# A transformer layer with routed experts: the loads of the first two tile pairs moved ahead of a block boundary

## The chip, the cores and the metric

The kernel runs on one core of one Trainium2 chip. The metric is the device time of one execution in microseconds (us), as the median of several runs.

## What is computed

One layer over 8 batches of 512 rows of 256 numbers: attention with 16 heads, then a feed-forward part with 16 experts, of which each row takes two, and a shared gated network. Cut to what matters here:

```python
x = x + layernorm(attention(layernorm(x)))
n = layernorm(x)
shared = (silu(n @ sfc1.T) * (n @ sfc2.T)) @ sfc3.T
top_w, top_idx = top_k(n @ gate_w.T, 2)          # per row
top_w = softmax(top_w)
dispatch[t, top_idx[t]] += top_w[t]
h = silu(einsum('td,ehd->teh', n, w1))           # 16 experts, 128 hidden
moe = einsum('teh,te,edh->td', h, dispatch, w2)
x = x + layernorm(moe + shared)
```

## The kernel before, in words

The program is three blocks, one after the other. In each, the five engines run their own lists of instructions and meet only by semaphores. Between two blocks stands a barrier (line 715): each engine drains, reports, and goes on when all five have reported.

1. The attention block.
2. The merged stage (lines 1032 to 1418). It projects the attention's result, normalises, computes the gate and the ranks of the rows, and does the first five batches of the shared network. Each row is written twice, once per chosen expert, into `records` in HBM (`rows_in` in the code), sorted by expert: a record is 256 numbers, the row's weight and its destination. GpSimd writes them with indirect scatters (`scatter`, lines 1095 to 1110), 64 in all, and waits for them at line 1123. When the counts are known, SP pads the end of each expert's region with one tile of empty records: 16 DMAs out of `pad` at line 1084, at addresses read from `counts_i`. Its last wait (line 1086, `zeroed`) is for their landing. VectorE makes the tables with the expert and the first record of every tile (`tables_i`, line 1285); from then on they are in SBUF. The stage ends with the last pieces of the shared network on TensorE and ScalarE's copy of two banks into `O` (`keep`, line 1145).
3. The expert stage (lines 1420 to 1792). 80 tiles of 128 records are taken in 40 pairs, both tiles of a pair side by side. For pair s SP loads the two tiles from `records` into `rows[s % 9]` (line 1483), at addresses from `tables_i`, which it reads 16 at a time (line 1478). TensorE transposes pair s + 1 (line 1750), ScalarE rounds it (line 1569), VectorE takes the rest (line 1669), and TensorE multiplies with the first expert weights (line 1768). TensorE reads its own table of experts, 16 at a time, at line 1743, in the step after the first transposes. Silu, another transpose and the second product (line 1780) follow, ScalarE scales the result (line 1583), and GpSimd scatters it to `rows_out` (line 1518). The last three batches of the shared network and the closing normalisation come behind it. SP waits at line 1487 until all scatters have landed before it reads them back.

The order of the work around the change is that of SP's list: 16 paddings, the wait for them, the barrier, a load of 16 registers, then the row loads of pairs 0 to 8 with no wait, and from pair 9 on each pair behind the scatter of the pair nine before it (`sent`). The tiles `rows[0]` to `rows[4]` lie in the memory of `projected`, `rows[5]` to `rows[8]` in memory of their own (`m_rows`). The first 2048 columns of `projected`'s memory hold the output projection, the gate's weights and the bias during the merged stage, and the constants of the ranks stand behind them.

```python
            sp.wait_ge(weights_in, 16 * B)
            sp.wait_ge(zeroed, 16 * E)
```

Of the kernel before, what the change touches and what calls it, by code (L numbers as in the profile page):

```python
# [5 lines left out]
B, N, D, H, HD = 8, 512, 256, 16, 16  # L6
P = 128
# [3 lines left out]
ROW = D + 2  # L11
# [7 lines left out]
RECORDS = E * REGION + E * P  # L19
# [9 lines left out]
F32 = mybir.dt.float32  # L29
# [707 lines left out]
def tiles(T, b):  # L737
    return T[:, b * QT:(b + 1) * QT, :]
# [7 lines left out]
def feed_forward(nc, ctx, iota_in, upper_in, split, rows_in, rows_out, out, X, O_rows, ident, pad, before):  # L746
# [3 lines left out]
    def sb(name, shape, dt=F32):  # L750
        return ctx.enter_context(nc.sbuf_tensor(name, shape, dt))

    def sem(name):
        return ctx.enter_context(nc.semaphore(name))
# [20 lines left out]
    pairs = projected[:, :, :, :].rearrange("p k c n -> p (k c n)")  # L775
# [7 lines left out]
    def part(T, c0, n):  # L783
# [16 lines left out]
    gate_s, lt_s, lg_s, gap_s, ratio_s, taken_s, route_s, both_s, wts_s, rank_s, slot_s = (  # L800
        asem(x) for x in "gate lt lg gap ratio taken route both wts rank slot".split())
    first_rows, copied, scattered = ([asem(f"{x}{i}") for i in range(2)] for x in ("first_rows", "copied", "scattered"))
    total_s, summed_s, table_s, end_s, inverse_s, counts_s, turned_s, zeroed, weights_in = (
        asem(x) for x in "total summed table end inverse counts turned zeroed weights_in".split())
# [223 lines left out]

    experts = sb("experts", [P, S1 // P, 2, P], F32R)
    tables_i = sb("tables_i", [2, TILES], I32)  # L1030

    with ExitStack() as sub:

# [27 lines left out]
        def sync(sp):  # L1061
            sp.dma_start(upper, upper_in).then_inc(consts_in, 16)
            sp.dma_start(iota[:, :], iota_in).then_inc(consts_in, 16)
            whole = whole_of(experts)
            for b in range(B):
                if b == B - 1:
                    sp.wait_ge(gate_s, B - 2)
                sp.dma_start(whole[:, 2 * b:2 * b + 2], split_v[:, 2 * b:2 * b + 2]).then_inc(weights_in, 16)
                sp.wait_ge(x2_s, (b + 1) * QT)
                sp.wait_ge(wts_s, b + 1)  # L1070
                if b == 0:
                    sp.wait_ge(consts, 3)
                for i in range(2):
                    t = b * QT + 2 * i
                    if b > 0:
                        sp.wait_ge(scattered[i], 32 * b)
                    sp.dma_start(second_rows[i][:, :, 0:D], O[:, t:t + 2, :]).then_inc(copied[i], 16)
                    sp.dma_start(second_rows[i][:, :, D:ROW], extra[:, t:t + 2, :]).then_inc(copied[i], 16)
            sp.wait_ge(counts_s, 1)
            at_r = [sp.alloc_register(name=f"count_at{e}") for e in range(E)]  # L1080
            sp.load(at_r, counts_i[0:1, :])
            for e in range(E):
                at = sp.snap(at_r[e], min_val=e * REGION, max_val=(e + 1) * REGION - P)
                sp.dma_start(rows_in[bass.ds(at, P), :], pad[:, :]).then_inc(zeroed, 16)
            sp.wait_ge(weights_in, 16 * B)
            sp.wait_ge(zeroed, 16 * E)

        def gpsimd(pool):
            nc.gpsimd.iota(O_rows[:, :, D + 1:ROW].bitcast(U32), pattern=[[P, NT], [0, 1]], base=0, channel_multiplier=1).then_inc(consts, 1)
# [240 lines left out]
        def tensor(pe):  # L1330
# [83 lines left out]
            for m in range(2 * LAST, EARLY * SC):  # L1414
                first(m)
                second(m - 1)
            second(EARLY * SC - 1)
        run_block(nc, sync=sync, gpsimd=gpsimd, scalar=scalar, vector=vector, tensor=tensor)

    with ExitStack() as sub:  # L1420
# [5 lines left out]
        msem = lambda name: sub.enter_context(nc.semaphore("m_" + name))  # L1426
        PAIRS = TILES // 2
        LOADS, HELD = 9, 4
        loaded, sent = ([msem(f"{x}{i}") for i in range(LOADS)] for x in ("loaded", "sent"))
        xt_s, xhi_s, xlo_s, mh_s, pre_s, msilu_s, gt_s, ghi_s, glo_s, my_s, scaled_s = (  # L1430
            msem(x) for x in "xt xhi xlo h pre silu gt ghi glo y scaled".split())
        x_out, added, pair_s, whole_s, res_s, last_out, shifted = (msem(x) for x in "x_out added pair whole res last_out shifted".split())
# [36 lines left out]
        def all_sent(engine):  # L1469
            for i in range(LOADS):  # L1470
                engine.wait_ge(sent[i], sends(i))

        def sync(sp):
            AT = 16
            at_r = [sp.alloc_register(name=f"row_at{j}") for j in range(AT)]
            for s in range(PAIRS):
                if 2 * s % AT == 0:
                    sp.load(at_r, tables_i[1:2, 2 * s:2 * s + AT])
                if s >= LOADS:
                    sp.wait_ge(sent[s % LOADS], 32 * (s // LOADS))  # L1480
                for f in range(2):
                    at = sp.snap(at_r[(2 * s + f) % AT], min_val=0, max_val=RECORDS - P)
                    sp.dma_start(rows[s % LOADS][:, f, :], rows_in[bass.ds(at, P), :]).then_inc(loaded[s % LOADS], 16)
            for b in ROWS[:ADDED]:
                sp.dma_start(out_v[b], tiles(X, b)).then_inc(x_out, 16)
            sp.wait_ge(my_s, PAIRS)
            all_sent(sp)
            for j, b in enumerate(ROWS):
                sp.dma_start(picked[:, j, :, :], moe_v[0, b]).then_inc(loaded[j], 16)
                if j < PLAIN:  # L1490
                    sp.dma_start(second[:, j, :, :], moe_v[1, b]).then_inc(loaded[j], 16)  # L1491
            for j in range(ADDED, B):
                for h in range(2):
                    at = ROWS[j] * QT + 2 * h
                    sp.wait_ge(res_s, 2 * (j - ADDED) + h + 1)
                    sp.dma_start(out_v[ROWS[j]][:, 2 * h:2 * h + 2, :], X[:, at:at + 2, :]).then_inc(last_out, 16)
            sp.wait_ge(last_out, 16 * 2 * (B - ADDED))
# [202 lines left out]
        def tensor(pe):  # L1700
# [82 lines left out]
            for i in range(EARLY, B):  # L1783
                pe.wait_ge(lo_s, (i - EARLY + 1) * DC)
                first(i * SC)
                for n in range(1, SC):
# [3 lines left out]
                    second(i * SC + n - 1)  # L1790
                second(i * SC + SC - 1)
        run_block(nc, sync=sync, gpsimd=gpsimd, scalar=scalar, vector=vector, tensor=tensor)


def transformer_layer(nc, x, w_qkv, w_out, b_out, gate_t, experts_t, cos, sin, ident_in, iota,
                      upper, steps, rows128, rows_in, rows_out, out):
    with ExitStack() as ctx:
        X = ctx.enter_context(nc.sbuf_tensor("X", [P, NT, D], F32))
        O_rows = ctx.enter_context(nc.sbuf_tensor("O", [P, NT, ROW], F32))
        pad = ctx.enter_context(nc.sbuf_tensor("pad", [P, ROW], F32))  # L1800
        ident = ctx.enter_context(nc.sbuf_tensor("identity", [P, P], F32))
        records = nc.dram_tensor("records", (RECORDS, ROW), F32, kind="Internal").ap()
        split = nc.dram_tensor("split", (CHUNKS, P, SC, 2, P), F32, kind="Internal").ap()

        def before(banks, held_parts, qk, v_first, halves, norm_parts, ahead):
            with ExitStack() as sub:
                sync, gpsimd, scalar, vector, tensor = attention(
                    nc, sub, x, w_qkv, cos, sin, ident_in, rows_in, records, split, (experts_t, w_out, gate_t, b_out), X, O_rows,
                    ident, pad, banks, held_parts, qk, v_first, halves, norm_parts, ahead)
                run_block(nc, sync, gpsimd, scalar, vector, tensor)  # L1810

        with ExitStack() as sub:
            feed_forward(nc, sub, iota, upper, split, records, rows_out, out, X, O_rows, ident, pad, before)
# [48 lines left out]
```

## Time and profile before

| what | us |
|---|---|
| median of 3 runs | 917.66 |
| lowest and highest of them | 910.24 and 919.96 |
| the profiled execution | 915.94 |
| its span, first to last instruction | 914.1 |
| mean granted TensorE clock over the span | 0.945 |

The merged stage's last instructions and the expert stage's first lie at about 712 us of the span. A row of a view shows the start in us from the span's start, how long it took, the engine, the line and the tiles; in brackets stands how long the engine was idle before it, and what ended that. "PEld" is TensorE's weight load, "SPq" and the like the instruction queue of an engine, where waits, branches and issues of DMAs are seen. A granted clock of 1.00 is 2.4 GHz, 0.50 is 1.2 GHz.

### The profile page before, as it was taken

The page shows a single profiled execution, that of the slowest core. Times are in us where ns is not written, and L with a number is a line of the kernel's source. Part 1 is how long each engine was busy: PE and PEld are TensorE (multiplying, and loading weights), DVE is VectorE, ACT ScalarE, POOL GpSimd, SP SyncE. Part 2 cuts the span into 40 slices and gives each one's busy share as a digit, 9 for nine tenths or more (in the row PEclk, how much of TensorE's full clock was granted, in tenths as well). Part 3 has the DMA queues.
Part 4 walks back from the last instruction along what each step waited for, and adds up shares of the span by engine and source line. Part 5 has one row for each costly group of instructions (what it writes and reads, how often), then busy time and mean ns, then how long its engine had stood idle before and what let it go on. Part 6 is the DMA issues. An engine that isn't in the chain of part 4 may idle for free. (4 is left out here: it accounts for less than half of the span.)

```text
span 914.1 us, 14969 instructions
## 1 busy us (share of the span) xinstructions
PE 776.8 (85%) x4690; PEld 479.2 (52%) x4690; DVE 650.4 (71%) x1256; ACT 520.9 (57%) x1047; POOL 372.9 (41%) x442
## 2 busy tenths in 40 slices
PE   4578798998998989989978877999999788888784
PEld 3433343343443433434422336877877688877673
DVE  4488689688697888887878836778765455553775
ACT  1226577676676777766756754343442466665363
POOL 4430171451630814515300001565665076766442
PEclk9869899898998999989989999999999899999998
DMA  8966637727737568367275401354466355555994
GB/s 157 240 127 167 133 74 157 179 83 163 163 103 170 100 145 179 98 160 163 92 148 88 186 1 52 126 163 150 134 189 210 107 168 172 175 164 193 296 164 92
DMA packets 112421, 133.29 MB, mean 146 GB/s; under 512 B 16724, under 2 KB 80726, under 8 KB 112344
## 3 DMA queue, kind: packets, MB, share of 16 engines
q1 hardware_dynamic: 98616, 108.39, 47.5%
q0 software_dynamic: 13248, 23.15, 9.7%
q10 hardware_dynamic: 480, 0.79, 0.6%
q8 instruction: 40, 0.66, 0.3%
q14 instruction: 37, 0.30, 0.1%
HBM read 68.18 MB, written 59.87 MB: 140 GB/s over the span
## 5 line engine op out<-in xcount | busy, mean ns | idle before, releaser
L480 DVE TENSOR_REDUCE negmax<-ring 128x2 f32<-128x1024 f32 x256 | 306.7, 1212 | 90.4 <-PE ring L643 89.7
L430 ACT ACTIVATE probs<-scores 128x512 f32<-128x512 f32 x498 | 273.6, 599 | 117.3 <-PE scores L661 114.4
L661 PE MATMUL scores<-q_st,k_st 64*128 64x512 f32 x498 | 208.0, 477 | 29.2 <-DMA q_st<-max_rows 16.5
L643 PE MATMUL ring<-k_st,q_st 48*128 48x512 f32 x512 | 187.1, 482 | 26.1 <-issue 9.7
L661 PEld LDWEIGHTS scores<-q_st,k_st 64*128 64x128 f32 x498 | 84.3, 194 | 178.8 <-ACT probs L430 103.1
L675 PE MATMUL av<-probs,v_aug 128*32 128x512 f32 x1024 | 145.0, 640 | 6.3 <-ACT probs L430 6.3
L331 POOL CAST part_r<-negmax 128x16 fp32r<-128x16 f32 x32 | 7.6, 238 | 208.7 <-DVE negmax L480 208.7
L643 PEld LDWEIGHTS ring<-k_st,q_st 48*128 48x128 f32 x512 | 73.3, 199 | 36.7 <-issue 23.1
L166 POOL TENSOR_TENSOR scratch<-qk_raw,cos 128x512 f32<-128x512 f32 x29 | 37.1, 1278 | 82.9 <-ACT qk_raw L383 81.8
L1518 POOL DMA_INDIRECT rows_out<-m_y,projected x48 | 47.3, 985 | 48.1 <-ACT m_y L1583 37.7
L1669 DVE TENSOR_TENSOR m_h_lo<-scores,m_h_hi 128x512 fp32r<-128x512 f32 x40 | 27.6, 691 | 52.2 <-ACT m_h_hi L1569 52.0
L590 PE MATMUL misc<-projected,t_hi 128*128 128x256 f32 (+1 forms) x220 | 54.4, 338 | 0.0
L733 PE MATMUL scores<-a_t_hi,shared 128*128 128x512 f32 x128 | 45.2, 406 | 4.7 <-DVE a_silu L1185 4.2
L1569 ACT CAST m_h_hi<-scores 128x512 fp32r<-128x512 f32 x40 | 23.5, 587 | 42.6 <-PE scores L1750 42.6
L675 PEld LDWEIGHTS av<-probs,v_aug 128*32 128x32 f32 x1024 | 20.5, 109 | 48.6 <-issue 37.5
L1768 PE MATMUL ring<-experts,m_h_lo 128*128 x160 | 44.4, 309 | 0.2 <-DVE m_h_lo L1669 0.2
L169 POOL TENSOR_TENSOR scratch<-qk_raw,sin 128x256 f32<-128x256 f32 x58 | 42.1, 747 | 0.0
L590 PE MATMUL misc<-projected,t_lo 128*128 128x256 f32 (+1 forms) x110 | 41.2, 374 | 0.0
L1768 PE MATMUL ring<-experts,m_h_hi 128*128 x160 | 40.8, 286 | 0.0
L590 PEld LDWEIGHTS misc<-projected,t_hi 128*128 128x128 f32 x220 | 38.3, 194 | 3.4
L322 POOL TENSOR_TENSOR qk<-scratch 128x512 f32<-128x512 f32 x29 | 37.5, 1294 | 1.3
L1518 POOL DMA_INDIRECT rows_out<-m_y,m_rows x32 | 31.5, 985 | 13.8 <-issue 7.3
(253 smaller groups left out, 1635.3 us busy)
## 6 DMA issues: line engine op xcount, KB each, us to landing
q_st<-rows_in SPq DMA_DIRECT2D x96, 128.0 KB, 4.5
k_st<-rows_in SPq DMA_DIRECT2D x90, 128.0 KB, 5.5
experts<-split SPq DMA_DIRECT2D x8, 1024.0 KB, 6.0
projected<-records SPq DMA_DIRECT2D x48, 129.0 KB, 2.2
split<-O SPq DMA_DIRECT2D x24, 256.0 KB, 3.0
experts<-rows_out SPq DMA_DIRECT2D x10, 512.0 KB, 8.1
m_rows<-records SPq DMA_DIRECT2D x32, 129.0 KB, 2.4
X<-in_x SPq DMA_DIRECT2D x8, 512.0 KB, 5.0
```

The lines of the kernel that those rows point to most:

```text
L166: engine.tensor_tensor(heads(a), src, c, ALU.mult).then_inc(done, 1)
L169: engine.tensor_tensor(heads(b)[:, :, cols], src[:, :, 1 - half::2], sin[:, t, cols].unsqueeze(1).broadcast_to([P, 2 * H, 8]), ALU.mult).t ...
L322: nc.gpsimd.tensor_tensor(qk[b % 2][:, t, :], rope_a, rope_b, ALU.add).then_inc(qk_done, 1)
L430: nc.scalar.activation(probs[r // 2 % 2][r % 2][:, a, :], score_of(R)[:, a, :], ACT.Exp, scale=HD ** -0.5).then_inc(exp_done, 1)
L480: nc.vector.tensor_reduce(negmax[Gn % 2][:, t, 2 * p:2 * p + 2], ring[t % 2][:, :, :], AX.X, ALU.max, negate=True).then_inc(max_done, 1)
L590: last = nc.tensor.matmul(bank[:, k * width:(k + 1) * width], x[:, c, t * P:(t + 1) * P], w[:, c, cols], start=j == 0, stop=j == len(terms ...
L643: last = nc.tensor.matmul(half[:, a, :], q[rows, t * P:(t + 1) * P], k[rows, :], start=True, stop=True)
L661: nc.tensor.matmul(score_of(R)[:, a, :], k[rows, kt * P:(kt + 1) * P], q[rows, :], start=True, stop=True).then_inc(sc_ps, 1)
L675: last = nc.tensor.matmul(av[32 * i:32 * i + 32, :], v_aug[b % 2][:, kt, g * GH + i, :], probs[kt % 2][i // 2][:, i % 2, :], start=kt == 0 ...
L733: ins = nc.tensor.matmul(out_ap, a, b, start=first and k == 0, stop=last and k == n - 1, skip_group_check=True)
L1518: nc.gpsimd.indirect_dma_start(out=rows_out, out_offset=bass.IndirectOffsetOnAxis(ap=rows[s % LOADS][:, f, D + 1:ROW].bitcast(U32), axis=0 ...
L1768: last = nc.tensor.matmul(bank_a[s % 2][:, f * 2 * P:(f + 1) * 2 * P], x_part[s % 2][:, f, c, :], block, start=f == 0 and k == 0, stop=f = ...
```

## The change

SP's list in the merged stage gets the row loads of pairs 0 and 1 (two DMAs each) at its end, behind the wait for the padding. To have the addresses it waits for the tables (`counts_s`) and loads four registers from them. Since the loads write into `projected`'s memory, it also waits for the ranks, the total and the gate, and since they read `records`, for both kinds of scatter. The semaphores `loaded0` and `loaded1` are made outside the blocks, so that TensorE's wait in the next block can use them. In the expert stage SP leaves these four loads out; its register load stays.

```diff
+    first_loaded = [sem(f"loaded{i}") for i in range(2)]
+    first_tiles = pairs[:, 0:2 * 2 * ROW].bitcast(F32).rearrange("p (i f d) -> p i f d", f=2, d=ROW)
...
             sp.wait_ge(weights_in, 16 * B)
+            sp.wait_ge(counts_s, 2)
+            tile_r = [sp.alloc_register(name=f"first_tile{j}") for j in range(2 * len(first_loaded))]
+            sp.load(tile_r, tables_i[1:2, 0:2 * len(first_loaded)])
+            sp.wait_ge(rank_s, B)
+            sp.wait_ge(total_s, 1)
+            sp.wait_ge(gate_s, B)
+            for i in range(2):
+                sp.wait_ge(first_rows[i], 32 * B)
+                sp.wait_ge(scattered[i], 32 * B)
             sp.wait_ge(zeroed, 16 * E)
+            for i in range(len(first_loaded)):
+                for f in range(2):
+                    at = sp.snap(tile_r[2 * i + f], min_val=0, max_val=RECORDS - P)
+                    sp.dma_start(first_tiles[:, i, f, :], rows_in[bass.ds(at, P), :]).then_inc(first_loaded[i], 16)
...
-        loaded, sent = ([msem(f"{x}{i}") for i in range(LOADS)] for x in ("loaded", "sent"))
+        loaded = first_loaded + [msem(f"loaded{i}") for i in range(len(first_loaded), LOADS)]
+        sent = [msem(f"sent{i}") for i in range(LOADS)]
...
-                for f in range(2):
+                for f in range(2 if s >= len(first_loaded) else 0):
```

SP's list before, from the last padding through the barrier (lines 715 and 717) to the first row loads. ISA is the register operation that makes an address, `projected` the memory of the first row tiles:

```order
L1083 ISA
L1084 DMA records<-pad 128x258
L715 UNCONDITIONAL_BRANCH [waits a_zeroed,a_weights_in]
L717 UNCONDITIONAL_BRANCH [waits barrier_Pool_Activation_PE_DVE_SP_release]
L1478 TENSOR_LOAD tables_i
L1482 ISA
L1483 DMA projected<-records 128x258
```

The same place of the same list with the change (its lines stand 2 to 16 lower in the file). The address operation and the DMA of the three other early loads are left out, and so are the later ones:

```order
L1085 ISA
L1086 DMA records<-pad 128x258
L1090 TENSOR_LOAD tables_i [waits a_counts,a_weights_in]
L1100 ISA [waits a_scattered0,a_first_rows1,a_first_rows0,a_scattered1,a_gate,a_zeroed,a_total,a_rank]
L1101 DMA projected<-records 128x258
...
L715 UNCONDITIONAL_BRANCH
L717 UNCONDITIONAL_BRANCH [waits barrier_Pool_Activation_PE_DVE_SP_release]
L1494 TENSOR_LOAD tables_i
L1498 ISA
L1499 DMA projected<-records 128x258
```

Four row loads moved from behind the barrier to ahead of it, and a table load came in ahead of the wait for the padding. The lists of the other engines are unchanged.

## Rows read from the trace of the kernel before

**Rows 1.** TensorE's waits from 700 to 722 us: total, times, longest.

```profile
PE scores L1750 <- DMA projected<-records: 5.3, 1, 5.3
```

**Rows 2.** TensorE in order of time: start, us, line, operation, tiles, count, idle before.

```profile
710.77 0.39 PE L733 MATMUL misc<-shared,a_h_hi 128*128 128x256 f32 x2
716.48 1.11 PE L1750 MATMUL scores<-identity,projected 128*128 128x128 f32 x4 [5.31 <-DMA projected<-records]
717.84 1.09 PE L1750 MATMUL scores<-identity,projected 128*128 128x128 f32 x4 [0.24 <-issue]
719.10 0.58 PE L1768 MATMUL ring<-experts,m_h_lo 128*128 x1 [0.17 <-DVE m_h_lo L1669]
...
720.97 0.95 PE L1750 MATMUL scores<-identity,projected 128*128 128x128 f32 x4
...
722.70 0.60 PE L1750 MATMUL scores<-identity,projected 128*128 128x128 f32 x4
```

**Rows 3.** The barrier, line 715, 700 to 730: ns min/median/max, first and last start.

```profile
L715 POOLq DRAIN  x1: 5299/5299/5299, 706.3 to 706.3; - x1
...
L715 SPq DRAIN  x1: 7/7/7, 710.6 to 710.6; - x1
L715 ACTq DRAIN  x1: 1022/1022/1022, 711.3 to 711.3; - x1
L715 SPq EVENT_SEMAPHORE  x1: 17/17/17, 712.5 to 712.5; - x1
```

**Rows 4.** SP's row loads in order of time; landing of the first six.

```profile
713.71 5.10 SPq L1483 DMA_DIRECT2D projected<-records  x10
...
DMA to landing us min/median/max: 2.1/2.1/2.2
```

**Rows 5.** Instructions that read `tables_i`, whole span; columns as rows 3.

```profile
L1478 SPq TENSOR_LOAD <-tables_i x5: 969/1152/1356, 712.5 to 798.2; - x5
L1743 PEldq TENSOR_LOAD <-tables_i x5: 1155/1257/1301, 716.5 to 804.6; - x5
```

**Rows 6.** Stretches: us, busy (count) by engine, PEclk, DMA share, GB/s.

```profile
698.00:702.00 4.00, 3.55 (x22) 3.17 (x23) 2.75 (x10) 0.95 (x2) 3.14 (x3) 1.00 0.94 275
713.00:714.50 1.50, 0.00 (x0) 0.00 (x0) 0.00 (x0) 0.00 (x0) 0.00 (x0) 1.00 0.00 0
717.00:721.00 4.00, 3.58 (x16) 2.81 (x15) 1.39 (x2) 1.17 (x2) 0.00 (x0) 0.50 0.87 240
722.00:724.00 2.00, 2.00 (x19) 1.87 (x18) 1.33 (x3) 1.52 (x4) 0.00 (x0) 1.00 0.64 183
769.50:772.80 3.30, 3.30 (x18) 3.30 (x16) 1.72 (x3) 1.90 (x5) 1.63 (x2) 0.50 0.72 206
```

**Rows 7.** GpSimd's scatters, line 1518, and its waits for ScalarE: total, times, longest.

```profile
L1518 POOL DMA_INDIRECT rows_out<-m_y,projected x48: 983/985/996, 729.8 to 841.4; - x48
L1518 POOL DMA_INDIRECT rows_out<-m_y,m_rows x32: 983/985/994, 742.7 to 831.1; - x32
...
POOL rows_out L1518 <- ACT m_y L1583: 44.2, 22, 28.0
```

**Rows 8.** Padding (lines 1084, 1086) and scatters' end (line 1123); columns as rows 3.

```profile
L1084 SPq DMA_DIRECT2D records<-pad x16: 332/332/1565, 696.9 to 706.6; - x16
...
DMA to landing us min/median/max: 2.4/3.5/4.3
...
L1086 SPq EVENT_SEMAPHORE  x1: 17/17/17, 710.4 to 710.4; - x1
...
L1123 POOLq EVENT_SEMAPHORE  x1: 43/43/43, 706.1 to 706.1; - x1
```

**Rows 9.** TensorE in order of time: two shorter pauses; columns as rows 2.

```profile
698.45 0.38 PE L733 MATMUL av<-shared,a_h_lo 128*128 128x256 f32 x1 [1.82 <-DVE a_h_lo L1189]
...
768.87 0.66 PE L1750 MATMUL scores<-identity,projected 128*128 128x128 f32 x4 [1.91 <-DMA projected<-records]
```

## The prediction

> **What bounds the kernel now.** The stretch to read is the seam between two blocks: the end of the merged stage (projection, gate, ranks, the first five batches of the shared network) and the start of the expert stage. I read the waits of TensorE there first. They hold one long item: 5.3 us in which TensorE waits for a DMA out of the records [rows 1]. The order in time places it. The last matmul of the merged stage starts at 710.77 us and lasts 0.39, and the first transposes of the expert stage start at 716.48 [rows 2]. ScalarE and VectorE have nothing to do meanwhile, because their first work needs those transposes.
>
> The 5.3 us has two parts, which the barrier separates. Before it, ScalarE still copies the last banks: its drain starts at 711.3 and lasts 1.02 us, until 712.3; GpSimd's, from 706.3 for 5.3 us, is over at 711.6, SP's at 710.6; and SP is let go at 712.5 [rows 3]. Behind it, SP loads 16 registers from the table in 0.97 us, issues its first row load at 713.71, and the data of pair 0 is there at 716.48. So the way from the first issue to the first transpose is 2.77 us. Ten such loads are issued in 5.10 us, a pitch of 0.52, and they land 2.1 us after their issue [rows 4, 5]. Neither part is limited by bandwidth: between 713.0 and 714.5 no DMA engine moves anything [rows 6].
>
> What bounds the stage after it decides whether an earlier start is kept. GpSimd issues 80 scatters of 0.985 us there (48 plus 32). The first starts at 729.8, after one wait of 28.0 us for ScalarE's first scaled tile, and the last at 841.4, a pitch of 111.6 / 79 = 1.41; its further waits for ScalarE sum to 44.2 - 28.0 = 16.2 us [rows 7]. They are waits inside the stage's own loop (row buffers are reused nine pairs later). Nothing in the loop is tied to a moment outside the stage, and the closing stage starts only when all scatters have landed (line 1487). An earlier start therefore moves the whole rest of the program.
>
> **The change, part by part.** SP now issues the four loads of pairs 0 and 1 before the barrier, behind the wait for the padding.
>
> 1. *When they can go.* The last of 16 paddings is issued at 706.6 and they land in 2.4 to 4.3 us; SP's wait for them ends at 710.4. The other condition that could be late, the scatters, is met at 706.1, where GpSimd passes its own wait for them [rows 8]. The added waits on rank, total and gate are on matmuls done before the shared network's last pieces. So the padding stays last and the added waits cost nothing.
> 2. *The added table load* on SP (four registers) stands between the last padding issue and that 3.5 us wait. The two rows for such a load show 0.97 to 1.36 us [rows 5], so the wait covers it. Without this cover it would cost about 1 us.
> 3. *Pair 0.* First issue at 710.4 + 0.1 for the register operation = 710.5; plus 2.77 as before gives 713.3. The DMA engines are idle then too (landing of the padding has just ended), so I keep the same 2.77.
> 4. *The barrier.* Four issues at 0.52 keep SP until 710.5 + 2.1 = 712.6. Its drain came 0.2 after its wait before (710.4 to 710.6), so it arrives at 712.8 instead of 710.6. ScalarE arrives at 712.3. SP becomes the last, by 0.5 us, and all engines leave at 712.8 + 0.2 = 713.0 instead of 712.5. What is queued behind is only the new block, and TensorE, which needs pair 0 at 713.3, has 0.3 us to spare.
> 5. *First transposes.* They start at the later of 713.3 and 713.0, against 716.48. Gain 3.2 us.
> 6. *Pair 1.* TensorE loads its own table in 1.26 us right behind pair 0's transposes, and only then transposes pair 1 [rows 2, 5]. Shifted, that is 714.6. Pair 1's first load is issued at 711.5 and lands by the same 2.77 at 714.3. Hidden.
> 7. *Pair 2 and later.* SP leaves the barrier at 713.0, loads registers and issues pair 2's first load 1.2 us later (as 712.5 to 713.71 before), at 714.2; there by 717.0. TensorE wants it at 720.97 - 3.2 = 717.8. Hidden by 0.8 us. Each further pair is issued 2 x 0.52 = 1.04 us later and wanted 1.73 later (transposes at 720.97, then 722.70 [rows 2]), so the cover only grows.
> 8. *The four loads removed* from the new block free SP and cost nothing: SP waits for sent buffers afterwards in any case.
>
> **The clock.** TensorE's granted clock is 1.00 (2.4 GHz) until 714.5, is 0.50 (1.2 GHz) from 717 to 721, after 5.3 us without a matmul, and is 1.00 again from 722 [rows 6]. Four transposes take 1.11 us at the lower level and 0.60 at the higher [rows 2]. The shorter pause, 711.2 to 713.3, is 2.1 us. The trace has two pauses a little shorter than that: 1.82 us before 698.45, where the clock stayed at 1.00, and 1.91 us before 768.87, after which it was 0.50 from 769.5 [rows 6, 9]. With the sparse start (transposes, 1.3 us of table load, transposes again) I take it that the clock falls again. If it doesn't, TensorE is ready for pair 2 earlier: pair 1's transposes end at 714.6 + 0.6 = 715.2, and ScalarE and VectorE took 719.10 - 717.59 = 1.5 us behind the first ones [rows 2], which makes 716.7 instead of 717.8, but pair 2 is there only at 717.0. That caps the extra gain at 0.8 us.
>
> The Trainium skill, "TensorE: Matmul & The Clock Gate", section "HAM oscillation — how this bites in real kernels", says that a wait for DMA between two bursts drops the engine to half clock, so that the next burst starts slowly; by it, a wait cut short enough would give back the slow start too. That is the case just priced, 4.0 us in all, and the 768.87 row speaks against counting on it.
>
> **Sum.** Profiled execution 915.94 us, of which the span is 914.1. Less 3.2: 912.7. The median of the runs shown is 917.66 and their range 910.24 to 919.96; the four times, the profiled one included, average 915.95, so the profiled execution is a fair base. From the median the same step would give 914.5. The unknown with far ends is TensorE's readiness behind the barrier: it is hidden before by the load, so it lies anywhere from 713.0 to 716.48, a gain of 0 to 3.2. I take the early end, since SP's first instruction starts at its release (712.5) in the same barrier.
>
> **Rivals.**
> - *The clock stays up.* 4.0 us, 911.9. For it: the pause falls from 5.3 to 2.1 us. Against: row 768.87.
> - *TensorE isn't ready.* Something that the load hid (fetching the new block's code, its first register work) ends at about 716. Then nothing is gained: 915.9. For it: the trace shows no event on TensorE between 712.5 and 716.48. Against: SP's prompt start.
> - *Slower: SP holds the barrier.* A DMA issue of the padding took up to 1.57 us where the queue was full [rows 8]. If each of the four takes that plus 0.2, SP arrives at 710.5 + 7.1 + 0.2 = 717.8 and the others leave at 718.0. The first transposes come 1.5 us later than before: 917.4. It decides from the point where SP arrives after 716.3, an issue of 1.4 us each. Against: the wait for the padding empties the queue first, and the ten loads before took 0.52 each.
> - *The change doesn't do what it says.* If the padding landed 3.2 us later than here, the loads would go at the same time as before. It landed while no other DMA ran, so I give it no chance of its own.
>
> **How the numbers follow.** The forecast (912.7) has 0.62, the clock staying up 0.19, TensorE not ready 0.11, SP holding the barrier 0.08. All lie within 911.9 to 917.4. The runs of the kernel before already differ by nearly 10 us, so the range is set by these: about 5 us either side, 907.5 to 918. A measurement of this kernel tells about 1%, 9.2 us, from no change. No mechanism here is worth that, so faster by over 1% gets 0.05 and slower 0.03, both from the scatter of the runs; within 1%, 0.92.
>
> **What would show it.** Right: four loads issued at 710.5 to 712.1 on SP (times counted from the padding's landing), the barrier left 0.3 to 0.8 us later than ScalarE's drain plus 0.2, transposes 2.8 us after the first issue, the wait of 5.3 us down to about 2.1, pair 2 without a wait, the first scatter still 13.3 us behind the first transposes. Wrong: first transposes later than 714, a wait for pair 2, issues of over 1 us, or a scatter chain that ends no earlier although it starts earlier.

## The result and the profile after

| | before | after |
|---|---|---|
| median of 22 runs each, us | 911.88 | 907.52 |
| lowest and highest | 906.53 and 920.47 | 900.23 and 919.12 |
| profiled execution's span | 914.1 | 906.1 |
| mean granted clock | 0.945 | 0.949 |

The ratio of the changed kernel to the one before is 0.9945, with a 95% interval of 0.9922 to 0.9967: 5.0 us faster, between 3.0 and 7.1. That is under 1%, and clear of no change. Both medians lie below what the first three runs had suggested (917.66).

TensorE in order of time with the change. Columns as in [rows 2]; line 1766 is what line 1750 was:

```profile
707.68 0.39 PE L733 MATMUL misc<-shared,a_h_hi 128*128 128x256 f32 x2
709.85 0.66 PE L1766 MATMUL scores<-identity,projected 128*128 128x128 f32 x4 [1.77 <-DMA projected<-records]
711.21 0.64 PE L1766 MATMUL scores<-identity,projected 128*128 128x128 f32 x4 [0.70 <-DMA projected<-records]
712.01 0.58 PE L1784 MATMUL ring<-experts,m_h_lo 128*128 x1 [0.17 <-DVE m_h_lo L1685]
...
713.88 1.05 PE L1766 MATMUL scores<-identity,projected 128*128 128x128 f32 x4
...
715.86 0.60 PE L1766 MATMUL scores<-identity,projected 128*128 128x128 f32 x4
```

The two profiles are best laid over each other at the last matmuls of the merged stage (710.77 before, 707.68 after), because 3.1 us of the 8.0 between the spans already lie ahead of them, where no work was changed. Behind that mark the first transposes come at 2.17 us instead of 5.71 [rows 2], the first scatter at 15.1 instead of 19.0, and the end at 198.4 instead of 203.3. So the start of TensorE gains 3.5 us, the way to the first scatter 0.4 more, and the 184 us behind it 1.0 more.

SP and the barrier with the change: its wait for the padding (line 1097), the four early loads (1101), and the barrier (715). Columns as in [rows 3]:

```profile
L1097 SPq EVENT_SEMAPHORE  x1: 28/28/28, 706.9 to 706.9; - x1
```

```profile
L1101 SPq DMA_DIRECT2D projected<-records x4: 332/338/370, 707.2 to 708.8; - x4
```

```profile
L715 POOLq DRAIN  x1: 5299/5299/5299, 703.7 to 703.7; - x1
...
L715 ACTq DRAIN  x1: 1022/1022/1022, 708.2 to 708.2; - x1
L715 SPq DRAIN  x1: 133/133/133, 709.2 to 709.2; - x1
L715 SPq EVENT_SEMAPHORE  x1: 17/17/17, 709.4 to 709.4; - x1
```

The loads go out 0.3 us behind the end of the wait, ScalarE and SP reach the barrier within 0.2 us of each other, and all leave at 709.4. Pair 0 is there 2.65 us behind its first issue, at 709.85: its landing still decides, not the barrier.

Stretches with the change, columns as in [rows 6]:

```profile
708.00:709.50 1.50, 0.08 (x1) 0.00 (x0) 0.00 (x0) 1.07 (x2) 0.00 (x0) 1.00 0.75 198
711.80:715.00 3.20, 3.03 (x15) 2.99 (x15) 1.44 (x3) 0.61 (x2) 0.00 (x0) 0.50 0.89 235
716.00:720.00 4.00, 4.00 (x37) 4.00 (x36) 3.76 (x8) 2.35 (x6) 0.00 (x0) 1.00 0.70 196
```

The DMA engines are busy 0.75 of the time from 0.3 to 1.8 us behind the last matmuls, where before they moved nothing. The clock still falls, 4 us behind the last matmuls, but it is up again at 716, 8.3 us behind them, where before it was still down at 721, 10.2 us behind them [rows 6]. The trace-wide row of the scatters keeps its shape:

```profile
L1534 POOL DMA_INDIRECT rows_out<-m_y,projected x48: 983/985/1087, 722.8 to 833.7; - x48
```

From first to last that is 110.9 us, against 111.6 [rows 7].

### The profile page after: what moved, and what is told of

It reads as the page before. It is cut to its first block and busy times, and to the rows that moved or that the text cites. A ratio compares the mean times of both kernels' runs of the same rounds, so it can differ in the third digit from the quotient of the medians.

```text
span 906.1 us, 14973 instructions
## 1 busy us (share of the span) xinstructions
PE 773.7 (85%) x4690; PEld 478.2 (53%) x4690; DVE 650.3 (72%) x1256; ACT 521.4 (58%) x1047; POOL 372.6 (41%) x442
## 5 line engine op out<-in xcount | busy, mean ns | idle before, releaser
L661 PE MATMUL scores<-q_st,k_st 64*128 64x512 f32 x498 | 207.9, 477 | 29.5 <-DMA q_st<-max_rows 16.8
L675 PE MATMUL av<-probs,v_aug 128*32 128x512 f32 x1024 | 142.9, 631 | 6.3 <-ACT probs L430 6.3
```

Of the source, the lines that this page charges most:

```text
L661: nc.tensor.matmul(score_of(R)[:, a, :], k[rows, kt * P:(kt + 1) * P], q[rows, :], start=True, stop=True).then_inc(sc_ps, 1)
L675: last = nc.tensor.matmul(av[32 * i:32 * i + 32, :], v_aug[b % 2][:, kt, g * GH + i, :], probs[kt % 2][i // 2][:, i % 2, :], start=kt == 0 ...
```

## The experiments

Each kernel is the changed one unless said otherwise, and each has an edit of its own below. "Wait's end", "transposes", "scatter" and "end" are the end of SP's wait for the padding, TensorE's first transposes, GpSimd's first scatter and the end of the span, in us behind the last real matmuls of the merged stage (the mark), from the one profile of that kernel. Each group shares one chip and its runs of the kernel before: e1, e2, e3 and e6 on one chip, e7 to e10 on a second, e11 to e14 on a third, e15 to e17 on a fourth. On the first two of these chips the expert stage takes some 29 us longer, so "end" is compared only within the first two groups or within the rest. The ratio isn't the quotient of the two medians: for e17 that would be 0.9958, for e12 it is 0.9996 either way.

| kernel | wait's end | transposes | scatter | end | ratio, 95% interval |
|---|---|---|---|---|---|
| before, first profile | -0.4 | 5.7 | 19.0 | 203.3 | |
| after, first profile | -0.8 | 2.2 | 15.1 | 198.4 | 0.9945 (0.9922, 0.9967) |
| e1_hold | -1.5 | 5.5 | 18.9 | 231.5 | 1.0013 (0.9974, 1.0051) |
| e2_one_pair | -1.6 | 1.8 | 18.1 | 231.9 | 0.9984 (0.9948, 1.0020) |
| e3_three_pairs | -1.0 | 2.7 | 14.3 | 229.3 | 1.0003 (0.9971, 1.0036) |
| e6_warm | 0.2 | 3.1 | 15.0 | 228.0 | 0.9965 (0.9930, 1.0001) |
| e7_before_again | -0.4 | 5.8 | 18.9 | 232.6 | 1.0009 (0.9978, 1.0040) |
| e8_after_again | -0.5 | 2.6 | 16.5 | 228.9 | 0.9927 (0.9893, 0.9961) |
| e10_hold_again | -3.6 | 5.7 | 19.8 | 232.0 | 1.0011 (0.9977, 1.0044) |
| e9_table_ahead | -1.0 | 2.7 | 17.0 | 229.2 | 0.9987 (0.9948, 1.0027) |
| e11_before_busy | 0.6 | 5.9 | 17.5 | 201.4 | 0.9980 (0.9945, 1.0014) |
| e12_after_third | 0.9 | 4.0 | 17.8 | 199.2 | 0.9996 (0.9959, 1.0033) |
| e13_three_again | 0.4 | 4.1 | 18.0 | 199.3 | 1.0002 (0.9960, 1.0044) |
| e14_busy_again | 1.1 | 4.0 | 17.9 | 198.7 | 0.9983 (0.9941, 1.0025) |
| e15_split_wait | | 1.9 | 15.0 | 197.5 | 0.9938 (0.9901, 0.9974) |
| e16_split_three_busy | | 1.8 | 13.5 | 197.4 | 0.9947 (0.9917, 0.9977) |
| e17_after_fourth | -0.3 | 2.9 | 16.8 | 198.6 | 1.0005 (0.9972, 1.0038) |

The ratios are wide because the 700 us ahead of the seam spread: the mark itself lies between 704.2 and 715.7 us in sixteen of the profiles and at 723.7 in e1's. Measured from the mark, the profiles part cleanly. On the first two chips, the kernels that have both pairs early and use them (e3, e6, e8, e9) end 228.0 to 229.3 us behind it, and the others (e1, e2, e7, e10) 231.5 to 232.6. On the other chips the former end at 197.4 to 199.3, and the kernel before at 203.3 and, with the clock up (e11), at 201.4. So the profiles show the gain in all four executions of the changed kernel, in e12 and e17 too, whose ratios show none: 3.7 us in e8 against e7, and 4.1 to 4.9 against the one profile of the kernel before. They are one execution each.

### Is it TensorE's start? e1, e10 and e7

```diff
                     pe.wait_ge(loaded[x % LOADS], 32 * (x // LOADS + 1))
+                    if x == 0:
+                        pe.wait_ge(loaded[2], 32)
```

Expected of e1_hold:

> TensorE's first transposes also wait for pair 2, which is still loaded behind the barrier; all else is the changed kernel. Theory (the gain is the earlier start of TensorE and nothing else): first transposes about 5.7 us behind the last matmuls of the merged stage, as in the kernel before, the first scatter 18 to 19 us behind them instead of 15.1, and a time within 1.5 us of the kernel before (ratio 0.998 to 1.002). Rival (the gain comes from the loads no longer competing or from SP's shorter list in the expert stage): the ratio stays near 0.9945.

Expected of e10_hold_again:

> The changed kernel with TensorE's first transposes held until pair 2 is there. Theory: the gain of the changed kernel on the same chip goes away, ratio 0.998 to 1.002, first scatter 18.5 to 19.1 us behind the last matmuls. Rival: ratio as that of the changed kernel.

Expected of e7_before_again, the kernel before run as a kernel of its own:

> The kernel before itself, so that its parts can be laid beside those of the next three on the same chip. Every theory: ratio 1.000, first transposes 5.3 to 5.8 us and first scatter 18.5 to 19.1 us behind the last matmuls of the merged stage.

TensorE in e1_hold, in order of time, columns as in [rows 2]:

```profile
723.72 0.39 PE L733 MATMUL misc<-shared,a_h_hi 128*128 128x256 f32 x2
729.26 1.09 PE L1768 MATMUL scores<-identity,projected 128*128 128x128 f32 x4 [5.14 <-DMA projected<-records]
```

SP's early loads and everything else are as in the changed kernel, and the 5.5 us are back. Both runs of it give a ratio of 1.001, while e8_after_again, on the chip and beside the runs of e10, gives 0.9927 with an interval that doesn't touch it. The group of e1 has no run of the changed kernel, and the changed kernel of other groups gave 1.000 as well (below), so by the ratios this rests on e8 against e10 and e7. The profiles agree with it: e10 ends 232.0 us behind the mark, e7 232.6 and e8 228.9. So the gain is TensorE's earlier start. SP's shorter list and less competition among loads are left with 0.6 us at most in these profiles, and the ratios can't show so little. The first scatter of e10 came at 19.8, later than expected, because the clock was down for longer there (14.1 us from the first transposes to the scatter).

### How many pairs? e2, e3 and e13

```diff
-    first_loaded = [sem(f"loaded{i}") for i in range(2)]
-    first_tiles = pairs[:, 0:2 * 2 * ROW]...
+    first_loaded = [sem(f"loaded{i}") for i in range(1)]     # 3 in e3 and e13
+    first_tiles = pairs[:, 0:1 * 2 * ROW]...
```

Expected of e2_one_pair:

> Only pair 0 is loaded ahead of the barrier. Theory (the two steps add: pair 0 by 3.5 us, pair 1 must be there too): first transposes 2.2 us behind the last matmuls, second transposes not before 6 us behind them (register load 1.2 and load 2.8 behind the barrier) instead of 3.5, the first scatter about 17 us behind; gain 1.5 to 2.5 us. Rival (only pair 0 matters): first scatter 15.1 us behind, gain as with two pairs.

Expected of e3_three_pairs:

> Pairs 0 to 2 are loaded ahead of the barrier. Theory (two more issues keep SP 1.05 us longer and it is the last at the barrier): barrier left 0.8 to 1.1 us later, first transposes no later than 0.7 us after those of the changed kernel, no wait for pair 2, first scatter 15 to 15.9 us behind the last matmuls; ratio within 0.1% of the changed kernel. Rival (SP has slack at the barrier): first scatter 14.5 us behind, 0.6 us faster.

Expected of e13_three_again:

> Three pairs ahead of the barrier once more, beside the changed kernel. Theory (the third pair neither costs nor gains): same ratio as the changed kernel within 0.2%, barrier left 1 us later, first transposes 0.1 to 0.6 us later, no wait for pair 2. Rival (SP's longer hold of the barrier eats the gain): first transposes over 1.5 us later than in the changed kernel, ratio 0.3% or more above it.

TensorE in e2_one_pair, columns as in [rows 2]:

```profile
713.68 0.40 PE L733 MATMUL misc<-shared,a_h_hi 128*128 128x256 f32 x2
715.49 0.63 PE L1766 MATMUL scores<-identity,projected 128*128 128x128 f32 x4 [1.42 <-PEq L715]
719.42 1.12 PE L1766 MATMUL scores<-identity,projected 128*128 128x128 f32 x4 [3.30 <-DMA projected<-records]
```

Pair 0 alone starts TensorE 3.9 us earlier, as early as any kernel here, and then it stands 3.3 us waiting for pair 1. The first scatter is 0.8 us earlier where 2 us were expected; both pairs are needed. With three pairs the first scatter comes at 14.3 in e3, as its rival had it, 4.7 us before that of the kernel before, but at 18.0 in e13, and neither ratio shows a gain. The barrier row of e13 says why the start was late:

```profile
L715 ACTq DRAIN  x1: 1022/1022/1022, 706.4 to 706.4; - x1
L715 SPq DRAIN  x1: 133/133/133, 709.6 to 709.6; - x1
```

ScalarE is through at 707.4 and SP comes at 709.7: six issues behind a late padding hold everyone by 2.3 us. That e3, with its early scatter, has no gain in its ratio stays unexplained. Its profile does keep part of it: it ends 2.2 us nearer to the mark than e1's on the same chip.

### The clock. e6, e14 and e11

```diff
             second(EARLY * SC - 1)
+            pe.wait_ge(g_s, EARLY * SC)
+            pe.wait_ge(h_s, EARLY * SC)
+            for _ in range(4):
+                nc.tensor.matmul(bank_a[:, :], part(shared, 0, P)[1], shared_operand(EARLY * SC - 1)[0][:, 0, :], start=True, stop=True, skip_group_check=True)
```

e11 is the kernel before, with 14 such matmuls (other operands) ahead of the loop of the expert stage.

Expected of e6_warm:

> Four more matmuls of 128x512, whose result nobody reads, stand at the end of TensorE's list in the merged stage of the changed kernel; they fill 1.0 us of its pause. Theory (a fall of the clock costs 0.4 to 0.8 us at this start): no stretch at 0.50 between the last matmuls and 10 us behind them, the first product of pair 0 takes 1.0 us instead of 1.9, and pair 2's landing is then what its transposes wait for; first scatter 14.3 to 14.7 us behind the last real matmuls. Rival (the clock falls anyway): same granted clock and times as the changed kernel.

Expected of e14_busy_again:

> The changed kernel with four idle matmuls ahead of the barrier once more. Theory (they keep the clock up, worth 0.8 to 2 us): no stretch at 0.50 in the 15 us behind the last matmuls, first scatter 11.6 to 11.9 us behind the first transposes, ratio 0.1 to 0.2% under the changed kernel's. Rival: the clock falls in this run, or the ratio is that of the changed kernel or above.

Expected of e11_before_busy:

> The kernel before, with 14 matmuls of 128x512 (0.23 us apart), whose result nobody reads, at the start of TensorE's list in the expert stage, where it waits 3.9 us for pair 0 anyway. The loads are as before. Theory (a fall of the clock at this seam costs 1.5 to 2.3 us, more than the 0.8 that was priced): first transposes as before (5.6 to 5.8 us behind the last real matmuls), no stretch at 0.50 in the 15 us behind them, first scatter 11.6 to 11.9 us behind the first transposes instead of 13.1 to 14.1; gain 1.5 to 2.3 us, ratio 0.9975 to 0.9985. Rival (the fall costs 0.8 at most): first scatter 12.4 us behind the first transposes or more.

Stretches of e11_before_busy, columns as in [rows 6]:

```profile
706.00:709.00 3.00, 2.75 (x12) 2.29 (x13) 0.00 (x0) 0.00 (x0) 0.00 (x0) 1.00 0.17 42
710.00:716.00 6.00, 5.05 (x39) 4.48 (x40) 3.45 (x6) 2.78 (x6) 0.00 (x0) 1.00 0.89 246
716.00:720.00 4.00, 4.00 (x37) 4.00 (x37) 3.17 (x7) 2.29 (x7) 0.00 (x0) 1.00 0.51 141
```

The loads and the first transposes (5.9) are as before, and the clock stays at 1.00. From the first transposes to the first scatter it takes 17.5 - 5.9 = 11.6 us. In the kernel before, with the clock down, it took 13.3, and 13.1 in e7; in the two held kernels 13.3 (e1) and 14.1 (e10). So the fall costs 1.5 to 2.4 us at such a late start, two to three times what was priced. In the changed kernel the same stretch took 12.9, 13.9, 13.9 and 13.9 us: the clock falls in each of its four profiles, and against the 11.8 of e6, where it stayed up, that costs 1.1 to 2.1 us. The four extra matmuls went with it in e6 and didn't help in e14 (13.9), where pair 0 was 0.9 us later. And in e3, which has none of them, the clock stayed up as well (11.6):

```profile
716.00:728.00 12.00, 10.72 (x89) 10.18 (x89) 8.22 (x14) 6.35 (x16) 0.00 (x0) 1.00 0.60 163
```

The length of the pause doesn't decide it: the clock fell behind one of 1.77 us in the first profile of the changed kernel, and stayed up behind one of 2.31 us in e3. The price of the fall is shown; that four matmuls are a remedy is not. The ratio of e11 (0.998) is what 1.8 us would give, and its interval holds 1.

### TensorE's table. e9

e9 has three pairs early, as e3, and TensorE's first table load in the merged stage. Part of its edit:

```diff
+            pe.wait_ge(counts_s, 2)
+            pe.load(expert_at[0:16], tables_i[0:1, 0:16])
             second(EARLY * SC - 1)
...
-                if of(s) and 2 * s % AT == 0:
+                if of(s) and s > 0 and 2 * s % AT == 0:
```

> Pairs 0 to 2 loaded ahead of the barrier, and TensorE's first table load (1.26 us) moved into the merged stage, ahead of its last products, where it waits for VectorE anyway. Theory (the table load is the next thing that holds the start): second transposes 0.7 us behind the first ones instead of 1.4, the first product of pair 0 unchanged at 2.2 us behind the first transposes, pair 2 without a wait; first scatter 14.0 to 14.4 us behind the last matmuls, ratio 0.993 to 0.996. Rival (the table load is hidden by ScalarE's and VectorE's work on pair 0): first scatter as with three pairs alone, 14.3.

```profile
717.48 1.07 PE L1771 MATMUL scores<-identity,projected 128*128 128x128 f32 x8 [2.27 <-PEq L715]
719.61 0.58 PE L1789 MATMUL ring<-experts,m_h_lo 128*128 x1 [1.07 <-DVE m_h_lo L1690]
```

These rows are TensorE's in order of time. Both pairs are transposed in one go, and the first product comes 2.13 us behind them, as in the changed kernel (2.16), bound by VectorE. On the first scatter it is inconclusive, since the clock fell in this profile.

### The same kernel again, and the padding. e8, e12, e17 and e15

Expected of e8_after_again:

> The changed kernel itself. Theory (an earlier start is kept to the end): first scatter 15.1 us behind the last matmuls (14.3 if the clock stays up), and from the first scatter to the end as long as in the kernel before on this chip, within 1 us; ratio 0.994 to 0.997. Rival (part of the gain is given back, or more is won, in the expert stage): the stretch from the first to the last scatter differs by over 2 us from that of the kernel before.

Expected of e12_after_third:

> The changed kernel once more. Theory (the gain is the earlier start, 2.4 to 3.9 us by the clock's fall, plus nothing): ratio 0.995 to 0.998, first scatter 15.1 to 16.6 us behind the last matmuls. Rival (more is won somewhere else): ratio under 0.994 again with the first scatter no earlier than that.

Expected of e17_after_fourth:

> The changed kernel beside these two. Theory: first transposes 2.9 to 3.1 us behind the end of SP's wait for the padding, wherever that falls (1.6 us ahead of the last matmuls to 1.1 us behind them so far); ratio 0.994 to 0.998. Rival: first transposes at a fixed 2.2 us behind the last matmuls, whatever the padding.

Three more measurements of the changed kernel gave 0.9927, 0.9996 and 1.0005. The interval of the first lies below that of the last and barely touches that of the second (0.9961 against 0.9959). The first transposes ranged from 2.2 to 4.0 us behind the mark. SP's wait in e12 ends at 716.6:

```profile
L1097 SPq EVENT_SEMAPHORE  x1: 28/28/28, 716.6 to 716.6; - x1
```

and its TensorE, in order of time, shows the last matmuls at 715.66 and pair 0 only then:

```profile
715.66 0.40 PE L733 MATMUL misc<-shared,a_h_hi 128*128 128x256 f32 x2
719.62 0.76 PE L1766 MATMUL scores<-identity,projected 128*128 128x128 f32 x4 [3.56 <-DMA projected<-records]
```

In the four profiles of the changed kernel the transposes come 2.95, 3.07, 3.02 and 3.16 us behind the end of the wait. So e17's theory holds at the seam, and its rival, a fixed 2.2, falls; its ratio, and that of e12, came out above what was expected, that of e8 below. By its ratio e8 gains 6.9 us, more than the seam and all behind it show (3.7), and e12 and e17 gain nothing, less than their profiles show: single groups of twelve runs don't settle half a per cent here. In e12 the first scatter came at 17.8 instead of 16.6 at the latest, behind first transposes at 4.0.

From the first scatter to the end e8 takes 0.4 and 0.9 us less than e7 (140.3 and 140.7 to the last scatter, 72.1 and 73.0 behind it), so an earlier start is kept there too.

What spreads is the padding. In the third group of kernels its median landing is 4.2 to 4.4 us instead of 3.5 [rows 8], and in e10 its last issue was 7.8 us ahead of the mark instead of 3.8 to 4.8; why, no run shows. In the kernel before this didn't matter, as the wait ended ahead of ScalarE's drain anyway, and that ended 1.5 to 1.6 us behind the mark in every profile. In e12 SP came 1.7 us behind ScalarE:

```profile
L715 ACTq DRAIN  x1: 1022/1022/1022, 716.2 to 716.2; - x1
L715 SPq DRAIN  x1: 133/133/133, 718.8 to 718.8; - x1
```

e15 puts the wait for 12 of the 16 paddings behind the early loads:

```diff
-                sp.dma_start(rows_in[bass.ds(at, P), :], pad[:, :]).then_inc(zeroed, 16)
+                sp.dma_start(rows_in[bass.ds(at, P), :], pad[:, :]).then_inc(first_zeroed if e < 4 else zeroed, 16)
...
-            sp.wait_ge(zeroed, 16 * E)
+            sp.wait_ge(first_zeroed, 16 * 4)
...
                     sp.dma_start(first_tiles[:, i, f, :], rows_in[bass.ds(at, P), :]).then_inc(first_loaded[i], 16)
+            sp.wait_ge(zeroed, 16 * (E - 4))
```

> The changed kernel, but the loads of pairs 0 and 1 wait only for the padding of experts 0 to 3 (and for all scatters, as before); SP waits for the other 12 paddings behind them, ahead of the barrier. This holds only where the first four tiles belong to the first four experts. Theory (the padding's landing sets how early pair 0 is there, and it spreads over 2.6 us between runs): loads issued 3.5 to 4.5 us ahead of the last matmuls of the merged stage, SP at the barrier by 1.2 us behind them, so that ScalarE is the last again and the first transposes come 1.8 to 2.1 us behind the last matmuls in every run; ratio 0.2% below the changed kernel's beside it. Rival (the loads land late because they share the DMA engines with the padding): first transposes at 2.9 us or later.

TensorE in e15_split_wait, in order of time, and its barrier, columns as in [rows 3]:

```profile
707.55 0.39 PE L733 MATMUL misc<-shared,a_h_hi 128*128 128x256 f32 x2
709.40 0.63 PE L1768 MATMUL scores<-identity,projected 128*128 128x128 f32 x4 [1.46 <-PEq L715]
```

```profile
L715 SPq DRAIN  x1: 13/13/13, 707.5 to 707.5; - x1
L715 ACTq DRAIN  x1: 1022/1022/1022, 708.1 to 708.1; - x1
L715 SPq EVENT_SEMAPHORE  x1: 17/17/17, 709.3 to 709.3; - x1
```

TensorE waits for nothing but the barrier now, which ScalarE sets again, and starts at 1.85, 3.9 us before the kernel before. The ratio is 0.9938, and e17 beside it gives 1.0005.

e16 adds the third pair and the four idle matmuls.

> As e15_split_wait, with three pairs loaded early and four idle matmuls at the end of TensorE's list in the merged stage. Theory: first transposes 1.8 to 2.1 us behind the last real matmuls, no stretch at 0.50 in the 15 us behind them, pair 2 without a wait, first scatter 13.4 to 13.9 us behind them, against 15 to 18 in the changed kernel; ratio 0.993 to 0.996. Rival (the stage gives it back): first scatter as early, and the time no lower than the changed kernel's.

Stretches of e16_split_three_busy, columns as in [rows 6]:

```profile
716.00:720.00 4.00, 2.64 (x15) 1.70 (x15) 0.69 (x1) 2.07 (x4) 0.00 (x0) 1.00 0.38 108
720.00:728.00 8.00, 8.00 (x70) 7.87 (x69) 6.49 (x11) 4.63 (x13) 0.00 (x0) 1.00 0.71 195
```

The clock stays up and the first scatter comes at 13.5 us, 5.5 us before that of the kernel before. The ratio, 0.9947 with a median of 904.27 beside 911.91, can't be told from e15's. Both beat the kernel before clearly. Against the changed kernel beside them the medians are 1.9 and 3.8 us lower, but the intervals of the ratios meet (e15's ends at 0.9974, e17's begins at 0.9972), so that they beat the changed kernel is likely and not shown. From the mark both end 1.2 us earlier than e17. Both rest on the first tiles belonging to experts 0 to 3; a kernel for any routing needs another way to have the padding early.

## Why the prediction was right or wrong

The forecast was 912.7 and the measured median is 907.52. The mechanism held and two terms of the sum were off.

- **The step that failed: the base of the sum.** The profiled execution's 915.94 was taken as fair, by four values that average 915.95. Of 22 runs the median is 911.88. That is 4.1 of the 5.2 us between forecast and measurement. The remaining 1.1 is the other term: the medians lie 4.4 us apart where the sum took off 3.2. The measured median lies at the very edge of the stated range.
- **The bound at the seam: right.** The wait of 5.3 us fell to 1.8. Putting it back (e10) takes the whole gain away on its chip.
- **The sum, "less 3.2": right for the place, wrong as one number.** The first transposes gained 3.5 us in the first pair of profiles. But item 1 took the end of the wait at 710.4, 0.4 us ahead of the last matmuls, as given. It lies between 3.6 ahead and 1.1 behind in other executions, and the gain of the changed kernel at this place, against the 5.7 of the first profile, is 3.5, 3.1, 1.7 and 2.8 us. One row of one execution stood for a time that spreads with the landing of the padding.
- **The gain in the whole time: undersized, within the noise.** 3.2 us were forecast, and 5.0 measured, between 3.0 and 7.1. Weighted by their intervals, the four measurements of the changed kernel average 0.9962, or 3.5 us; as they don't agree among themselves, that is rough. That the forecast's size comes out so well is in part luck, as its end of the wait and its price of the clock were both off.
- **The clock, "caps the extra gain at 0.8": wrong.** It falls again, as taken. The fall costs 1.5 to 2.4 us at the late start (e11) and 1.1 to 2.1 at the early one (e6), because it also slows the products behind pair 2's transposes and not only the way to them. How long it lasts differs between executions: about 3.4 us in the first profile of the changed kernel, which gave it 0.4 us on top, and about 6.8 in e8, where the way to the first scatter took 0.6 us more than in the kernel before.
- **The barrier, item 4: right in its mechanism, and underrated as a rival.** SP arrived with ScalarE in the first profile and 1.7 us behind it in e12. "SP holds the barrier" was priced by slow issues of 1.4 us. They took 0.5 as forecast; late padding is what makes SP late, and it makes pair 0 late too. That a full queue made the one issue of 1.57 us slow, as the prediction says, is shown by no row.
- **TensorE ready behind the barrier: right.** In e2 and e15 it starts 0.1 us behind its release.
- **Pair 2 and the carry: right.** Pair 2 isn't waited for, and 110.9 us from the first to the last scatter stand against 111.6. On the chip of e7 and e8 it is carried too, with 140.3 against 140.7.
- **The chances.** "Within 1%" came true. That the scatter of single runs says how much a change of 0.5% can be told from none did not: 22 runs of each told it.

## What to carry to other kernels

When loads are moved ahead of a barrier, ask what they now wait for. Here the first transposes came 3.0 to 3.2 us behind that event, so the gain is the distance from the event to the old start, less those 3 us. If the event is the landing of other DMAs, it spreads by microseconds between executions, where ScalarE's drain, which set the barrier before, stayed within 0.1 us of its place. Waiting only for what the first tiles need took another 0.3 to 2.1 us off the first transposes (e15); what that is worth in the whole time isn't settled. A pause of TensorE costs its length plus 1.1 to 2.4 us here if the clock falls behind it, so a shorter pause behind which it still falls gives back little more than the length. When a change is worth half a per cent, take the base from many runs, and measure from a mark just ahead of the changed place.

## What was not expected of the hardware

The kernel before took 911 to 912 us in three groups of measurements and 950 to 952 in two others (e1 to e10), on two other chips. Of the 31.6 us between the spans of its two profiles, 29 lie in the expert stage: in e7_before_again the scatters run from 732.0 to 872.7.

```profile
L1518 POOL DMA_INDIRECT rows_out<-m_y,projected x48: 982/985/997, 732.0 to 872.7; - x48
```

```profile
POOL rows_out L1518 <- ACT m_y L1583: 72.2, 15, 31.1
```

The first row is GpSimd's scatters (columns as in [rows 7]), the second its waits for ScalarE from 725 to 875 us. The scatters themselves are as short as before (985 ns), and 41 us of waits for ScalarE stand where there were 16 [rows 7]. ScalarE and VectorE pause there for 2 to 5 us at a time. Most of TensorE's pauses, up to 2.8 us, end with a tile of ScalarE, and what holds ScalarE the trace doesn't show. Nothing was tried on it. So the description of this stage as a chain of scatters doesn't hold on that chip. The gain at the seam is of the same size there.
